# Deferring two groups of fp32 transposes by one step in an attention-and-FFN layer kernel

## What is computed

```python
xn = _layernorm(x, axis=-1)                     # x: 16 x 2048 x 1024, fp32
s = attn(xn, Wq, bq, Wk, bk, Wv, bv, Wo, bo, gamma, beta)
#   q, k, v = split_heads(xn @ W + b)           16 heads of 64
#   att = softmax(causal(q k^T / sqrt(64)));  o = att @ v
#   y = o @ Wo + bo, then layernorm(y) * gamma + beta
g = _silu(ffn(xn, w_gate, w_up, w_down))        # 1024 -> 3072 -> 1024, int weights / 127
x = x + s * g
```

## Time and profile before

| | us |
|---|---|
| median of two timed runs | 7799.41 |
| the two runs | 7924.62, 7674.2 |
| the profiled execution | 7078.29 |
| its span on the slowest core (core 3) | 7076.7 |
| spans of the eight cores | 7028.1 to 7076.7 |
| TensorE busy in the span | 5744.2 |
| granted TensorE clock, mean of the cores | 0.893 to 0.899 |

### The profile page before, as it was taken

How to read it: one execution, slowest core, us unless ns; L and a number is a source line. 1 busy time by engine, 2 the same in 40 slices (tenths; PEclk the granted TensorE clock), 3 DMA queues, 4 the chain that set the end, 5 groups by cost and what they waited for, 6 DMA issues and landing times.

```text
span 7076.7 us, 79636 instructions; the slowest of 8 cores (7028.1 to 7076.7 us)
## 1 busy us (share of the span) xinstructions
PE 5744.2 (81%) x30072; PEld 2860.0 (40%) x30072; DVE 1369.0 (19%) x2330; ACT 1691.8 (24%) x3084; POOL 55.2 (1%) x108
## 2 busy tenths in 40 slices
PE   1478878877887586999895799899999985999998
PEld 1123323322322234676673333233333333766765
DVE  3202201201211123121122221122110114212111
ACT  4132232232232111111112234332333311111111
POOL 0000000000000000000000000000000000000000
PEclk9978888888888698999997798888999887999999
DMA  6411111111111334666665100000000032667666
GB/s 173 136 27 24 24 30 24 26 29 26 26 27 20 69 84 100 158 154 153 155 156 149 47 14 7 14 15 13 13 13 9 5 97 66 155 147 163 155 147 146
DMA packets 1512815, 529.73 MB, mean 75 GB/s; under 512 B 1384182, under 2 KB 1474550, under 8 KB 1512444
## 3 DMA queue, kind: packets, MB, share of 16 engines
q1 hardware_dynamic: 1390332, 419.75, 25.6%
q10 hardware_dynamic: 107136, 69.22, 3.2%
q0 software_dynamic: 14976, 35.66, 2.8%
HBM read 474.19 MB, written 69.21 MB: 77 GB/s over the span
## 4 chain that ended last, share of the span: by engine, by line
PE 74%; DMA 12%; DVE 5%; ACT 4%; issue 4%; SPq 1%; ACTq 0%; DVEq 0%; POOLq 0%
PE pb L780 15%; PE pb L555 10%; PE pb L1043 10%; PE pb L1031 9%; PE pb L733 8%; DMA pool_b<-scr_wblk 5%; PE pb L1107 5%; PE pb L607 5%; PE pb L909 5%; PE pb L672 2%; DMA scr_wblk<-pool_b 1%; PE pb L742 1%; SPq L105 1%; DMA pool_f<-x 1%; ACT pool_f L808 1%
## 5 line engine op out<-in xcount | busy, mean ns | idle before, releaser
L780 PE MATMUL pb<-pool_f 128*65 128x512 f32 (+3 forms) x2560 | 1155.6, 581 | 0.0
L757 ACT ACTIVATE pool_f<-pb,tiny 128x512 f32<-128x512 f32 (+3 forms) x1280 | 755.7, 622 | 1465.9 <-PE pb L742 1018.5
L1031 PE MATMUL pb<-arena_a,pool_b 128*128 128x256 bf16 x6144 | 738.5, 274 | 176.5 <-DMA pool_b<-scr_wblk 176.2
L555 PE MATMUL pb<-arena_a,pool_b 128*128 128x512 bf16 x3072 | 715.8, 392 | 159.0 <-DMA pool_b<-scr_whilo 159.0
L1107 PE MATMUL pb<-pool_b 128*128 128x512 bf16 x3072 | 694.1, 383 | 111.9 <-DMA pool_b<-scr_wblk 111.6
L1043 PE MATMUL pb<-arena_a,pool_b 128*128 128x256 bf16 x6144 | 735.9, 273 | 12.4 <-ACT pool_f L1120 10.9
L733 PE MATMUL pb<-pool_b 64*128 64x512 bf16 (+3 forms) x3840 | 708.8, 389 | 0.3 <-ACT pool_f L757 0.3
L1031 PEld LDWEIGHTS pb<-arena_a,pool_b 128*128 128x128 bf16 x6144 | 601.9, 98 | 255.6 <-issue 183.5
L1043 PEld LDWEIGHTS pb<-arena_a,pool_b 128*128 128x128 bf16 x6144 | 601.0, 98 | 88.4 <-issue 17.6
L780 PEld LDWEIGHTS pb<-pool_f 128*65 128x65 f32 x2560 | 326.1, 148 | 516.2 <-issue 496.2
L555 PEld LDWEIGHTS pb<-arena_a,pool_b 128*128 128x128 bf16 x3072 | 299.4, 100 | 564.0 <-issue 247.0
(11 more groups left out here) (84 smaller groups left out, 2676.2 us busy)
## 6 DMA issues: line engine op xcount, KB each, us to landing
pool_b<-scr_wblk SPq DMA_DIRECT2D x1152, 256.0 KB, 3.4
pool_f<-x SPq DMA_DIRECT2D x96, 512.0 KB, 4.4
pool_b<-scr_o SPq DMA_DIRECT2D x64, 512.0 KB, 5.6
pool_b<-scr_whilo SPq DMA_DIRECT2D x96, 256.0 KB, 4.0
scr_wblk<-pool_b ACTq DMA_DIRECT2D x72, 256.0 KB, 2.6
scr_whilo<-pool_b ACTq DMA_DIRECT2D x64, 256.0 KB, 3.0
scr_o<-pool_b ACTq DMA_DIRECT2D x128, 128.0 KB, 1.8
y<-pool_f ACTq DMA_DIRECT2D x32, 512.0 KB, 3.6
```

Of the source, the lines that this page charges most:

```text
L555: e.matmul(o, l, r, start=st, stop=sp)),
L757: e.activation(d, s_, AF.Exp, bias=bc)),
L780: e.matmul(o, l, r, start=st, stop=sp)),
L1031: e.matmul(o, l, r, start=st, stop=sp)),
```

## The change

It touches the order of two loops, and no operation, shape, buffer or transfer.

- In the apply pass everything of a tile that follows `v6` (the transposes, `hi`, `lo`) goes into a function `flush_atr`, called one tile later: the streams get v6(tt+1) first and then the transposes, `hi` and `lo` of tile tt. The last tile is flushed behind the loop.
- In the V projection the four transposes and the copy `evv` of a chunk go into `flush_vtr`, called one chunk later: TensorE's stream has the 24 matmuls of chunk tc+1 before the transposes of chunk tc, and VectorE's has `ev` of chunk tc+1 before `evv` of chunk tc. The last chunk is flushed behind the loop. `vfm_cons` and `v2_cons` become one-element lists so that the function can change them.

```diff
-        for tt in range(16):
-            s = tt % 2
-            tok = w.dma("sync", xt[s][:, :],
...
+        apend = []
+
+        def flush_atr(item):
+            s, tt, v6 = item
             for g2_ in range(2):
                 bank = pb[(tt * 2 + g2_) % 6]
...
+        for tt in range(16):
+            s = tt % 2
+            tok = w.dma("sync", xt[s][:, :],
+                        A(x_in, (b * T + tt * 128) * D, [[D, 128], [1, D]]),
+                        waits=xt_cons[s], sem=ld_x[s])
+            xt_cons[s] = []
+            v6 = w.op("scalar", (lambda e, d=xnt[s], x_=xt[s], tt=tt:
...
+                      waits=[tok, s3] + xn_cons[s], inc=c_se)
+            xt_cons[s] = [v6]
+            xn_cons[s] = []
+            apend.append((s, tt, v6))
+            if len(apend) > 1:
+                flush_atr(apend.pop(0))
+        while apend:
+            flush_atr(apend.pop(0))
...
+            vpend = []
+
+            def flush_vtr(item):
+                tc, ev = item
+                bankt = pb[2 + tc % 2]
+                tks = []
+                for j in range(4):
+                    tks.append(w.op("tensor",
...
+                                    waits=[ev] + pbk_cons[2 + tc % 2], inc=c_te))
+                pbk_cons[2 + tc % 2] = []
+                vfm_cons2[0].append(tks[-1])
+                evv = w.op("vector",
...
+                           waits=[tks[-1], v2ones] + v2_cons2[0], inc=c_ve)
...
-                          waits=[mmt] + vfm_cons, inc=c_ve)
+                          waits=[mmt] + vfm_cons2[0], inc=c_ve)
+                vfm_cons2[0] = []
                 pbk_cons[tc % 2].append(ev)
...
+                vpend.append((tc, ev))
+                if len(vpend) > 1:
+                    flush_vtr(vpend.pop(0))
+            while vpend:
+                flush_vtr(vpend.pop(0))
```

More of the change, by code:

```diff
@@ L438, in build_program @@
                 aa_done.setdefault(tt // 4, []).append(lo)
+        for tt in range(16):
[5 more added lines that the diff above has]
+            v6 = w.op("scalar", (lambda e, d=xnt[s], x_=xt[s], tt=tt:
+                                 e.activation(d[:, :], x_[:, :], AF.Identity,
+                                              bias=rb16[:, tt:tt + 1],
+                                              scale=r16[:, tt:tt + 1])),
+                      waits=[tok, s3] + xn_cons[s], inc=c_se)
[6 more added lines that the diff above has]
+            flush_atr(apend.pop(0))
         if b == 0:
@@ L477, in build_program @@
         linvb_cons2 = [[]]
+        vfm_cons2 = [[]]
+        v2_cons2 = [[]]
         kq_cons = [[], []]
@@ L480, in build_program @@
         ksq_cons = [[], []]
-        vfm_cons = []
-        v2_cons = []
         att_cons = [[[], []], [[], []]]
@@ L593, in build_program @@
                 flush_mhat(mhat_pend.pop(0))
+            vpend = []
[5 more added lines that the diff above has]
+                    tks.append(w.op("tensor",
+                                    (lambda e, o=bankt[:, j * 128:(j + 1) * 128],
+                                     s_=vfm[:, (tc * 4 + j) * 128:(tc * 4 + j + 1) * 128]:
+                                     e.transpose(o, s_, idf_s[:, :])),
+                                    waits=[ev] + pbk_cons[2 + tc % 2], inc=c_te))
+                pbk_cons[2 + tc % 2] = []
+                vfm_cons2[0].append(tks[-1])
+                evv = w.op("vector",
+                           (lambda e, tc=tc, s_=bankt:
+                            e.tensor_copy(
+                                V2.rearrange("p (tt g j) -> p tt g j", g=2, j=65)
+                                [:, tc * 4:(tc + 1) * 4, :, 0:64],
+                                s_[:, 0:512].rearrange("p (tt g j) -> p tt g j",
+                                                       g=2, j=64))),
+                           waits=[tks[-1], v2ones] + v2_cons2[0], inc=c_ve)
+                v2_cons2[0] = []
+                pbk_cons[2 + tc % 2].append(evv)
+                v2cons.append(evv)
             for tc in range(4):
@@ L823, in build_program @@
                          for t in att_cons[sl2][hh]]
-            v2_cons = [t for hh in range(2) for sl2 in range(2)
-                       for t in att_cons[sl2][hh]]
+            v2_cons2[0] = [t for hh in range(2) for sl2 in range(2)
+                           for t in att_cons[sl2][hh]]
             v2cons = []
-            vfm_cons = vfm_cons + lrow_cons[0] + lrow_cons[1] + linvb_cons2[0]
+            vfm_cons2[0] = vfm_cons2[0] + lrow_cons[0] + lrow_cons[1] + linvb_cons2[0]
             negm_cons = [exp_toks[k] for k in exp_toks][-1:]
```

## The result

| | before | after |
|---|---|---|
| median of the timed runs | 7584.91 us (10 runs) | 6918.39 us (11 runs) |
| fastest run | 7068.29 us | 6908.96 us |
| profiled execution, span of its slowest core | 7076.7 us | 6915.2 us |

The ratio is 0.9776, 95% interval 0.9757 to 0.9796: 2.2% faster.

The account below looks back on a forecast made before the run. TensorE, busy 5744 of 7077 us, was taken as the bound, so only its 1333 us of idleness or the clock could give time. 62 + 35 = 97 us off the 7799 us median gave 7702 us, range 6940 to 7840.

Parts of the forecast that it names:

- V projection: Transposes issued one chunk later remove waits at chunk boundaries: 3.9 us per round, 16 rounds, 62 us (bounds 56 to 65).
- Apply pass: Normalization issued ahead of the previous tile's copies: 2.85 us per tile instead of 4.02, 35 us for two batch elements.
- The clock: Low-clock stretch behind L653 may shift either way, 38 us at most; taken as nothing.
- the clock helps: Rival: fuller end of V keeps the clock up behind L653; 151 us in all, 7648 us, chance 0.10.
- The slower rivals: Denser V makes the chip lower the clock in V itself: net 7994 us, +2.5%, chance 0.04.
- the rule of a lowered die: Skill's warning: a peak-current limiter lowers a die's clock once three cores run dense matmuls; FFN row spoke against it.
- The level: 97 us taken off the median of two timed runs, 7799 us; chance 0.10 that timed runs fall to another level.

## Why the prediction was wrong

- **V projection, 62 us: right.** 65.1 us. The chunk takes 5.62 us, so the 0.2 us of overlap counted as probable were there; the gap in front of the last transposes covered those of chunk 2; and the copy fitted into VectorE's slack, L653 waiting 1.26 us as before.
- **Apply pass, 35 us: right.** 36.9 us. The load of x took over as the limit at about 2.8 us per tile, the pace of the statistics pass (2.85), and the gain went through the weight split. The version with four buffers shows both.
- **The clock, 0 us, at most 38 either way: the step that failed.** It was 45.5 us, beyond the bound, and for two reasons. I priced only the 20 us behind L653 (0.78 against 0.66), where a round wins 2.4 us of work. A round of the second element won 6.2 us (136.6 to 130.4), since the three low intervals further on also halved: the clock's later falls come at moved instants of the query blocks too. And I called the sign open, though the trace pointed one way: of the sixteen rounds of core 3 in the kernel before, eleven had the long low interval (13.6 us) and five the short one, so a shift had more to gain than to lose.
- **The rival "the clock helps" had the right size and the wrong mechanism.** It gave 151 us in all (160 measured) by a fuller end of V. The runs with superfluous matmuls show that the filling did not bring the gain and the shift of 4.1 us did; that the number came near is luck.
- **The slower rivals did not come.** In 800 us of the changed kernel's FFN the clock stayed at 0.99, and V's matmuls lost nothing (403 ns each, before and after). But one trace was too little to set the rule of a lowered die aside: the 0.81 named under the result is such a lowering. Runs with the mean clock of a die that low came with the kernel before as with the changed one, so it does not speak for this rival.
- **The level.** 7702 us put the effect on the level of two timed runs, 721 us above the profiled execution, and this is most of the distance to 6918. Six of the eleven timed runs of the changed kernel came out at the level of the profiled execution, which had been 0.10 of the chances; with one fewer the median would have been some 350 us higher, so that it fell below the range is in part luck of the draw. The low end of the range allowed 138 us off that level, and 160 came off, by the size of the clock term.

## What to carry to other kernels

A wait of an in-order engine for a result that another engine makes of its work is removed by issuing the waiting instructions one step later; read its worth from the timeline, with the overlap of the pipeline's end, and ask at once what is late next (here the load, whose remedy is a third and fourth buffer). Where TensorE is often at the low clock, a change of a few us ahead of a sparse stage shifts that stage against the clock, which here gained 45 us and, with three matmuls more, lost 67, next to the 102 of the waits themselves: try a version with a few superfluous matmuls before a result is put down to an edit. And count an engine's pace from start to start, not as a sum of durations.

## What the runs showed of the hardware

- The granted clock depended on when the work came, not only on what it was: 3 matmuls more per round in the changed kernel (11 us of work) cost 67 us on the mean of the cores, 13 more in the kernel before (44 us) cost nothing, with the order of everything else the same.
- In the kernel before, the query blocks alone spend 977 us of the 7053 at the low clock, and the change took 120 of them away. V's matmuls start every 427 ns at the low clock and every 216 at the high one (medians on core 3). The Trainium skill (TensorE: Matmul & The Clock Gate, Part 1) puts the penalty of the clock's ramp below 1% of a typical kernel's span. That speaks of the ramp alone; the 977 us show that it can't stand for all low-clock time of a kernel whose sparse stages recur.
- ScalarE's neighbouring instructions overlapped at their ends, by 0.22 us behind a 128x1024 activation, and a 512 KB load of x took about 4.5 us from issue to landing with two buffers as with four.
